# A gated attention and MLP block: means subtracted on GpSimd, weights rounded on VectorE, shares and order of the work set anew

## What is computed

```python
n  = layernorm(x)                                   # over the last axis, no gain or bias
qp = (n @ W1.T + b1) @ W2.T + b2;  kp = (c @ W1.T + b1) @ W2.T + b2
p  = softmax(qp @ kp.T / sqrt(128) + mask)          # mask [128, 120], added
x  = x + tanh(g_xattn) * (p @ c)
h  = relu(q8(q8(layernorm(x)) @ q8w(w1).T + q8w(b1)))   # 128 -> 512
x  = x + tanh(g_ffn) * (q8(h) @ q8w(w2).T + q8w(b2))    # 512 -> 128
# q8: round(16 v) clipped to -128..127, / 16;  q8w: round(64 v) clipped, / 64
```

## Time and profile before

| | |
|---|---|
| runs, us | 66.5, 66.66, 66.83; median 66.66 |
| profiled execution | 66.68 us, span 64.9, granted TensorE clock 1.0 |
| TensorE busy | 57.8 us (89%), weight loads 45.9 |
| VectorE busy | 54.7 us (84%), 308 instructions |
| ScalarE busy | 52.4 us (81%), 145 instructions |
| GpSimd busy | 44.5 us (69%), 92 instructions |
| DMA | 9.09 MB; the load queue is busy until some 20 us |

### The profile page before, as it was taken

How to read it: one execution, slowest core, us unless ns; L and a number is a source line. 1 busy time by engine, 2 the same in 40 slices (tenths; PEclk the granted TensorE clock), 3 DMA queues, 4 the chain that set the end, 5 groups by cost and what they waited for, 6 DMA issues and landing times.

```text
span 64.9 us, 1898 instructions
## 1 busy us (share of the span) xinstructions
PE 57.8 (89%) x565; PEld 45.9 (71%) x565; DVE 54.7 (84%) x308; ACT 52.4 (81%) x145; POOL 44.5 (69%) x92
## 2 busy tenths in 40 slices
PE   4999799768999899999999999999999899996830
PEld 4988574517877788795979899699696779464510
DVE  4569959496999899999799999999999998888620
ACT  2600889849999979999999999999999969769600
POOL 5958888994790894698999999906997949133000
PEclk9999999999999999999999999999999999999999
DMA  0899999999980000000000003120300403041232
GB/s 0 231 412 405 416 414 406 414 400 408 406 324 23 0 0 5 10 0 0 10 0 0 0 5 119 58 111 0 128 34 0 169 8 144 18 162 73 93 121 81
DMA packets 3324, 9.09 MB, mean 140 GB/s; under 512 B 369, under 2 KB 754, under 8 KB 3314
## 3 DMA queue, kind: packets, MB, share of 16 engines
q1 hardware_dynamic: 3312, 8.98, 35.9%
q10 hardware_dynamic: 2, 0.00, 0.0%
HBM read 6.88 MB, written 2.10 MB: 138 GB/s over the span
## 4 chain that ended last, share of the span: by engine, by line
POOL 38%; issue 14%; DMA 14%; ACT 10%; DVE 9%; PE 4%; SPq 4%; POOLq 1%; ACTq 1%; DVEq 0%
POOL xq L377 17%; DMA load_sb<-in_packed 14%; POOL rs L359 12%; ACT pr L597 4%; POOL xn L367 4%; SPq L326 4%; DVE st L641 3%; POOL rs L355 2%; ACT prT L606 2%; PE bank_A L483 2%; DVE load_sb L707 2%; PE bank_O L524 2%; ACT xn L573 1%; DVE mv L644 1%; ACTq L149 1%
## 5 line engine op out<-in xcount | busy, mean ns | idle before, releaser
L624 ACT ACTIVATE h<-bank_H,fb_q 128x512 int8<-128x512 f32 (+2 forms) x28 | 16.2, 645 | 2.2 <-PE bank_H L509 2.1
L641 DVE BATCH_NORM_STATS2 st<-load_sb 128x6 f32<-128x128 f32 x64 | 14.0, 279 | 2.4 <-DMA load_sb<-in_packed 2.3
L359 POOL TENSOR_TENSOR rs<-ve,half 128x4 f32<-128x4 f32 (+2 forms) x9 | 8.5, 941 | 9.3 <-DVE nm L648 9.3
L597 ACT ACTIVATE pr<-sc,mn 128x120 f32<-128x120 f32 x32 | 12.4, 408 | 0.9 <-DVE mn L695 0.9
L377 POOL TENSOR_SCALAR xq<-load_sb,nm,rs 128x128 int8<-128x128 f32 x28 | 12.3, 456 | 0.8 <-POOL rs L359 0.2
L355 POOL TENSOR_TENSOR rs<-ve,half 128x4 f32<-128x4 f32 (+2 forms) x9 | 8.5, 942 | 2.6 <-DVE nm L648 2.6
L367 POOL TENSOR_SCALAR xn<-load_sb,nm,rs 128x128 f32<-128x128 f32 x22 | 9.6, 448 | 0.5
L467 PEld LDWEIGHTS bank_S<-kpT,xaT 128*128 128x128 f32 x64 | 8.1, 191 | 2.6 <-issue 2.3
L483 PE MATMUL bank_A<-load_sb,prT 120*128 120x128 f32 x64 | 9.1, 283 | 0.3 <-ACT prT L606 0.3
L707 DVE SCALAR_TENSOR_TENSOR load_sb<-bank_A,rec,load_sb 128x128 f32<-128x128 f32 x32 | 9.1, 343 | 0.4 <-DVE rec L700 0.3
L524 PE MATMUL bank_O<-w_q,h 128*128 128x128 bf16 x128 | 9.2, 219 | 0.2
(11 more groups left out here) (80 smaller groups left out, 102.0 us busy)
## 6 DMA issues: line engine op xcount, KB each, us to landing
load_sb<-in_packed SPq DMA_DIRECT2D x6, 496.0 KB, 8.0
out_y<-y_sb SPq DMA_DIRECT2D x6, 256.0 KB, 2.0
load_sb<-in_packed SPq DMA_DIRECT2D x2, 512.0 KB, 11.0
load_sb<-in_packed SPq DMA_DIRECT2D x1, 576.0 KB, 14.2
load_sb<-in_packed SPq DMA_DIRECT2D x1, 514.0 KB, 6.1
load_sb<-in_packed SPq DMA_DIRECT2D x1, 448.0 KB, 5.3
load_sb<-in_packed SPq DMA_DIRECT2D x1, 432.0 KB, 12.7
load_sb<-in_packed SPq DMA_DIRECT2D x1, 428.0 KB, 13.3
```

Of the source, the lines that this page charges most:

```text
L359: nc.gpsimd.tensor_tensor(rs2[:, of(g, n=1)], ve2[:, of(g, n=1)], half[:, of(g, n=1)], ALU.pow).then_inc(rs2_done, 1)
L597: nc.scalar.activation(pr[i][:, j, :], sc[i][:, j, :], ACT.Exp, scale=-1.0, bias=mn[:, of(g, j, 1)], accum_out=den[:, of(g, j, 1)]).then_i ...
L624: nc.scalar.activation(low_byte(h16[g % RING], hcols(c, g)), bank_H[c][:, cols(g)], ACT.Relu, bias=fb1_q[:, c:c + 1]).then_inc(h_act[c], 1)
L641: nc.vector.bn_stats(st[:, START[g] + j, :], x_of(g, j)).then_inc(st_done, 1)
```

## The change

Four things. nm is gone from both layer norms; GpSimd subtracts the mean itself, and scale_means computes -mean * rs in one instruction. scale_weights moves, with its three instructions, from ScalarE to VectorE. The shares differ in a few groups: normalise has 21 tiles on GpSimd (22 before), 5 on ScalarE (7), 6 on VectorE (3); quantise 25 on GpSimd (28), 7 on VectorE (4); of the relus 29 are on ScalarE (28) and 7 on VectorE (8). And DUE and FILLERS are new. On VectorE the front is now: stats1 of 0, fold_cp1, scale_means 0, stats1 of 1, fold_cp2, stats1 of 2, scale_means 1, normalise 1, scale_weights, stats1 of 3, row_maxima 0, normalise 2, stats1 of 4, row_maxima 1.

```diff
-XN_ON_POOL = [1, 2, 3, 2, 4, 3, 2, 3, 2]
-XN_ON_ACT = [2, 2, 1, 2, 0, 0, 0, 0, 0]
-XQ_ON_POOL = [1, 3, 4, 4, 4, 4, 4, 3, 1]
-RELU_ON_ACT = [4, 4, 3, 3, 2, 3, 3, 3, 3]
+XN_ON_POOL = [1, 2, 3, 2, 3, 4, 2, 3, 1]
+XN_ON_ACT = [2, 1, 0, 2, 0, 0, 0, 0, 0]
+XQ_ON_POOL = [0, 3, 4, 4, 3, 3, 4, 3, 1]
+RELU_ON_ACT = [4, 4, 3, 3, 3, 3, 3, 3, 3]
...
-    stats1=[375, 485, 715, 977, 1110, 1325, 1569, 2218, 3232],
-    scale_means=[620, 879, 970, 1562],
-    fold_cp1=[627],
-    scale_weights=[845],
-    fold_cp2=[848],
-    copy_keys=[1002, 1053, 1413, 1756, 2149, 2503, 2917, 3552, 4294],
-    row_maxima=[1244, 1470, 1921, 2513, 2868, 3151, 3630, 4255, 4573],
-    normalise_dve=[0, 0, 0, 0, 0, 1789, 2459],
-    quantise_dve=[2032, 2708, 0, 0, 0, 0, 0, 0, 5741],
+    stats1=[380, 590, 743, 1053, 1267, 1505, 1715, 2641, 3361],
+    fold_cp1=[479],
+    scale_means=[583, 868, 0, 1481],
+    fold_cp2=[715],
+    copy_keys=[837, 920, 1332, 1768, 2140, 2719, 3144, 3695, 4263],
+    normalise_dve=[0, 876, 1241, 0, 2144, 0, 2252, 0, 3967],
+    scale_weights=[901],
+    row_maxima=[1180, 1391, 1947, 2306, 2770, 3271, 3555, 4193, 4567],
+    quantise_dve=[2172, 2742, 0, 0, 4256, 4462, 0, 0, 5716],
...
-FILLERS = [8, 38, 19, 5]
+FILLERS = [6, 29, 2, 6, 4]
...
-                pool.wait_ge(ve1_done, 2 * end)
+                pool.wait_ge(ve1_done, end)
...
-                    nc.gpsimd.tensor_scalar(xn[g % RING][:, tile(j)], x_of(g, j), nm1[:, of(g, j, 1)],
-                                            rs1[:, of(g, j, 1)], ALU.add, ALU.mult).then_inc(xn_pool, 1)
+                    nc.gpsimd.tensor_scalar(xn[g % RING][:, tile(j)], x_of(g, j), mv1[:, START[g] + j, 0:1],
+                                            rs1[:, of(g, j, 1)], ALU.subtract, ALU.mult).then_inc(xn_pool, 1)
...
-                nc.vector.tensor_scalar(nm[:, at], mv[:, at, 0], -1.0, None, ALU.mult).then_inc(ve_done, 1)
...
-                dve.wait_ge(ve1_done, 2 * g + 2)
-                nc.vector.tensor_tensor(nr1[:, of(g, n=1)], nm1[:, of(g, n=1)], rs1[:, of(g, n=1)],
-                                        ALU.mult).then_inc(nr1_done, 1)
+                nc.vector.scalar_tensor_tensor(out=nr1[:, of(g, n=1)], in0=mv1[:, of(g, n=1), 0], scalar=-1.0,
+                                               in1=rs1[:, of(g, n=1)], op0=ALU.mult, op1=ALU.mult).then_inc(nr1_done, 1)
...
+            def scale_weights():
+
+                wait_load(dve, "mlp")
+                nc.vector.tensor_scalar(mp_8[:, :], mp_sb[:, :], W_SCALE, None, ALU.mult).then_inc(quant8, 1)
+                dve.wait_ge(row_in, 16)
+                nc.vector.tensor_scalar(fb2_8[:, :], row_sb[:, 2:2 + D], W_SCALE, None, ALU.mult).then_inc(quant8, 1)
+                dve.wait_ge(quant8, 1)
+                nc.vector.tensor_scalar(w1_q[:, :], mp_8[:, 0:C * P], 1.0 / W_SCALE, None, ALU.mult).then_inc(w1_up, 1)
```

More of the change, by code:

```diff
@@ L48 @@
 ]
-XN_ON_POOL = [1, 2, 3, 2, 4, 3, 2, 3, 2]
-XN_ON_ACT = [2, 2, 1, 2, 0, 0, 0, 0, 0]
-XQ_ON_POOL = [1, 3, 4, 4, 4, 4, 4, 3, 1]
-RELU_ON_ACT = [4, 4, 3, 3, 2, 3, 3, 3, 3]
+XN_ON_POOL = [1, 2, 3, 2, 3, 4, 2, 3, 1]
+XN_ON_ACT = [2, 1, 0, 2, 0, 0, 0, 0, 0]
+XQ_ON_POOL = [0, 3, 4, 4, 3, 3, 4, 3, 1]
+RELU_ON_ACT = [4, 4, 3, 3, 3, 3, 3, 3, 3]
 DUE = dict(
-    stats1=[375, 485, 715, 977, 1110, 1325, 1569, 2218, 3232],
[L60 to L63, removed]
-    scale_means=[620, 879, 970, 1562],
-    fold_cp1=[627],
[L66 to L70, removed]
-    scale_weights=[845],
-    fold_cp2=[848],
-    project_keys=[888, 951, 1282, 1638, 2040, 2394, 2796, 3438, 3893],
-    widen_weights=[973],
-    copy_keys=[1002, 1053, 1413, 1756, 2149, 2503, 2917, 3552, 4294],
-    scores=[1069, 1368, 1724, 2126, 2629, 2981, 3528, 4027, 4495],
-    negate_mask=[1157],
-    row_maxima=[1244, 1470, 1921, 2513, 2868, 3151, 3630, 4255, 4573],
[L79 to L86, removed]
-    normalise_dve=[0, 0, 0, 0, 0, 1789, 2459],
-    stats2=[1815, 2325, 2734, 3319, 3711, 4111, 4614, 5031, 5541],
-    copy_base=[1929],
-    rstd2=[1934, 2470, 3171, 3595, 4075, 4257, 4759, 5150, 5641],
-    quantise_dve=[2032, 2708, 0, 0, 0, 0, 0, 0, 5741],
[L92 to L108, removed]
@@ new lines @@
+    spread_gates=[371],
+    stats1=[380, 590, 743, 1053, 1267, 1505, 1715, 2641, 3361],
+    fold_mm1=[386],
+    fold_cp1=[479],
+    rstd1=[492, 728, 926, 1191, 1431, 1643, 1894, 2871, 3524],
+    scale_means=[583, 868, 0, 1481],
+    fold_mm2=[587],
+    normalise_pool=[588, 839, 1302, 1552, 1764, 2110, 2785, 3283, 3797],
+    normalise_act=[603, 990, 0, 1538],
+    transpose_x=[644, 997, 1414, 1845, 2216, 2809, 3248, 3817, 4347],
+    fold_cp2=[715],
+    copy_xT=[735, 1094, 1487, 1910, 2286, 2884, 3318, 3943, 4416],
@@ new lines @@
+    project_keys=[755, 818, 1164, 1558, 1990, 2551, 3033, 3388, 4104],
+    copy_keys=[837, 920, 1332, 1768, 2140, 2719, 3144, 3695, 4263],
+    normalise_dve=[0, 876, 1241, 0, 2144, 0, 2252, 0, 3967],
+    scale_weights=[901],
+    scores=[904, 1266, 1643, 2076, 2468, 3165, 3453, 4016, 4498],
+    copy_ident=[974],
+    gate=[1029],
+    widen_weights=[1046],
+    negate_mask=[1142],
+    row_maxima=[1180, 1391, 1947, 2306, 2770, 3271, 3555, 4193, 4567],
+    exponentials=[1219, 1614, 1986, 2373, 2934, 3425, 3790, 4300, 4723],
@@ new lines @@
+    transpose_probs=[1346, 1734, 2161, 2652, 3116, 3571, 3967, 4460, 4905],
+    fold_base=[1384],
+    copy_probsT=[1400, 1822, 2226, 2776, 3201, 3636, 4040, 4623, 5029],
+    attend=[1469, 1902, 2306, 2856, 3294, 3729, 4147, 4692, 5140],
+    reciprocals=[1473, 1840, 2388, 2632, 3352, 3761, 3956, 4488, 5224],
+    residual=[1637, 2038, 2529, 2984, 3448, 3844, 4290, 4804, 5246],
+    stats2=[1848, 2396, 2851, 3143, 3636, 4066, 4607, 4949, 5422],
+    rstd2=[2005, 2534, 2989, 3413, 3840, 4204, 4745, 5061, 5514],
@@ new lines @@
+    quantise_dve=[2172, 2742, 0, 0, 4256, 4462, 0, 0, 5716],
+    copy_base=[2194],
+    transpose_xq=[2265, 2784, 3536, 4079, 4540, 4880, 5186, 5464, 5735],
+    split_base=[2283],
+    copy_xqT=[2333, 2833, 3739, 4213, 4672, 4979, 5271, 5563, 5813],
+    hidden=[2397, 2942, 3850, 4369, 4757, 5049, 5341, 5628, 5866],
+    relu1=[2524, 3085, 4097, 4505, 4860, 5152, 5444, 5715, 5937],
+    relu0=[2578, 3365, 3980, 4445, 4801, 5093, 5385, 5666, 5899],
+    relu2=[2624, 3576, 4154, 4564, 4920, 5212, 5504, 5764, 5975],
@@ L109 @@
+    quantise_pool=[0, 2645, 3100, 3614, 3961, 4325, 4866, 5167, 5605],
+    relu3=[2671, 3258],
+    mlp_out=[2698, 3614, 4233, 4563, 4927, 5208, 5481, 5767, 5959],
+    result=[3092, 3775, 4395, 4734, 5065, 5357, 5649, 5888, 6077],
+    relu_dve3=[0, 0, 4000, 4499, 4884, 5159, 5504, 5744, 5941],
+    keep_warm0=[370.5],
+    keep_warm1=[586.5],
+    keep_warm2=[643.5],
+    keep_warm3=[754.5],
+    keep_warm4=[996.5],
 )
-FILLERS = [8, 38, 19, 5]
+FILLERS = [6, 29, 2, 6, 4]
 class Share(list):
@@ L215, in norm @@
         def norm(n):
[L216 to L220, removed]
+            return sb(f"st{n}", [P, B, 6]), sb(f"mv{n}", [P, B, 2]), sb(f"ve{n}", [P, B]), sb(f"rs{n}", [P, B])
+        st1, mv1, ve1, rs1 = norm(1)
+        st2, mv2, ve2, rs2 = norm(2)
         mn, den, rec = (sb(n, [P, B]) for n in ("mn", "den", "rec"))
@@ L357, in rstd2 @@
             def rstd2(g):
-                pool.wait_ge(ve2_done, 2 * g + 2)
+                pool.wait_ge(ve2_done, g + 1)
                 nc.gpsimd.tensor_tensor(rs2[:, of(g, n=1)], ve2[:, of(g, n=1)], half[:, of(g, n=1)],
@@ L376, in quantise_pool @@
                 for j in range(XQ_POOL[g]):
-                    nc.gpsimd.tensor_scalar(low_byte(xq16[g % RING], tile(j)), x_of(g, j), nm2[:, of(g, j, 1)],
-                                            rs2[:, of(g, j, 1)], ALU.add, ALU.mult).then_inc(xq_pool, 1)
+                    nc.gpsimd.tensor_scalar(low_byte(xq16[g % RING], tile(j)), x_of(g, j), mv2[:, START[g] + j, 0:1],
+                                            rs2[:, of(g, j, 1)], ALU.subtract, ALU.mult).then_inc(xq_pool, 1)
             def widen_weights():
@@ L553, in gate @@
                 nc.scalar.mul(tg_out[:, :], tg[:, 1:2], 1.0 / (ACT_SCALE * W_SCALE)).then_inc(tg_out_up, 1)
[L555 to L562, removed]
             def copy_base():
@@ L626, in relu @@
                 return stage
-            schedule(once=dict(scale_weights=scale_weights, copy_ident=copy_ident, gate=gate, negate_mask=negate_mask,
+            schedule(once=dict(copy_ident=copy_ident, gate=gate, negate_mask=negate_mask,
                                copy_base=copy_base),
@@ L637, in _, with layer_stats @@
             nc.vector.memset(h16[0][:, :].bitcast(F32), BYTE_PAIR).then_inc(bytes_up, 1)
-            def layer_stats(g, st, mv, ve, nm, scale, st_done, mv_done, ve_done):
+            def layer_stats(g, st, mv, ve, scale, st_done, mv_done, ve_done):
                 for j in range(TILES[g]):
@@ L712, in stats2 @@
                 dve.wait_ge(x2_done, START[g + 1])
-                layer_stats(g, st2, mv2, ve2, nm2, ACT_SCALE, st2_done, mv2_done, ve2_done)
```

(1 more changed line is left out.)

4 lines of the change are left out of this document (2 added, 2 removed).

## The result

The changed kernel takes 72.39 us (median of 4, 72.04 to 73.3) against 66.75 (median of 4): the ratio is 1.082, 95% interval 1.075 to 1.090. Forecast were 65.6 and faster. Its profiled execution took 72.44 us, span 70.6 (before 66.68 and 64.9). Some executions of most kernels here take 1 to 4 us longer than the rest: the ratios, and the executions called undisturbed, leave those out, the medians don't.

What follows compares the result with a forecast made beforehand. The prediction took ScalarE to bound the middle, VectorE close behind, with VectorE's queue in the front setting when it starts. A 1.7 us earlier start, 1.1 of it kept, gave 66.68 - 1.1 = 65.6 us; range 64.7 to 66.6.

Steps and rivals of the forecast that it cites:

- Negated means: Layer norms: VectorE loses 18 instructions, 1.3 us; GpSimd's subtract-and-multiply priced like add-and-multiply, 0.45 us each.
- The upper bound of 1.02: GpSimd's subtract-and-multiply: at most the power's 1.02 us for four elements in place of 0.45.
- The bound: Middle, 14.20 to 49.90 us: ScalarE bounds it, 0.48 us idle, VectorE close behind; GpSimd, 8.14 idle, does not.
- Weights: Front: three weight conversions moved from ScalarE to VectorE cost 1.92 us there, bounds 1.0 and 3.2.
- the third rival: Front: weights on VectorE run at twice the rate, about 1.0 us, first maxima wait only for the mask; 65.2 us, chance 0.2.
- The front made anew: Reordered start: ScalarE's first exponentials at 12.5 instead of 14.22, 1.7 us earlier; third set at 20.0 instead of 21.74.
- The middle: Third exponentials to 49.89: VectorE's net added work 0.65 us; lead kept between 0.65 and 1.56, taken as 1.1.
- The tail: Behind the middle: one relu of group 4 moves from VectorE to ScalarE, cost 0, or 0.58 us if the wait is gone.
- The sum: Whole kernel: 66.68 - 1.1 = 65.6 us, own range 65.0 to 66.0.
- The clock rival: Front: thinner filling halves TensorE's granted clock, keys and scores 2 to 3 us later, 69 us; chance 0.03.

Runs made afterwards that it cites:

- e3: Kernel before, with GpSimd subtracting the negated mean instead of adding it, operand kept: 75.0 and 75.3 us, ratio 1.128.
- e4: Kernel before, with GpSimd adding the mean out of the mean-variance pair instead of the negated mean: 66.65 us in one execution, 68.02 in the other.
- e8: Kernel before plus 48 GpSimd instructions behind all its work, each form three times at 128x128 and 128x512; only the forms' durations count, add-and-multiply 451 and 767 ns.
- e9: Changed kernel with VectorE's negated means restored, GpSimd adding, and TensorE's first instructions in the order of the kernel before: ratio to before 0.992.
- e10: e9 with VectorE writing negated mean and scaled variance by one instruction instead of two: undisturbed 65.6 to 66.0 us, ratio to before 0.986.
- e1: Changed kernel with VectorE writing the negated means again and GpSimd adding them: undisturbed 66.01 and 66.14 us, ratio to before 0.991; four of six 68.7 to 69.2.
- e5: e1 with more matmuls of zeros, FILLERS [6, 37, 14, 6, 14] instead of [6, 29, 2, 6, 4]: undisturbed 66.6 to 67.0 us; 7 of 12 executions long.
- e7: e1 with the three conversions of the MLP's weights back on ScalarE: four executions at 68.8 to 70.7 us.
- e11: e10 with six tiles given from VectorE to GpSimd in the middle: 64.75, 65.06 and 65.47 us, ratio to before 0.975; the other three 68.0 to 68.4.

## Why the prediction was wrong

**Negated means: the step that failed.** "I take no difference" for GpSimd's subtract-and-multiply, at 0.45. It takes 0.79 (0.34 more, 46 times). e3 isolates the operation, e4 clears the operand, e8 shows why the row I priced it from was the wrong neighbour: add-and-multiply is the exception among GpSimd's forms and not their rule. The upper bound of 1.02 held the truth, but I gave it neither a rival nor a part of the range. It would have been 46 x 0.57 = 26 us of GpSimd against 8.1 of idle in the middle: the largest price in the text with no chance at all. The trace of before could have warned: on 96 partitions by 128 columns GpSimd's cast took 0.29 and its tensor_tensor subtract 0.42, so its time already went by the operation.

**The bound.** "Not the bound: GpSimd idle 8.14 us in the middle" told how little GpSimd could bear: of 15.6 us more, the middle's idle took 7.4. And it was a weak reading even of before: idle time doesn't say that the rest of an engine's work keeps nobody waiting. The chain of waits on the page of before puts GpSimd first (line by line, its quantise alone 17%), and the prediction left it out:

```profile
POOL 38%; issue 14%; DMA 14%; ACT 10%; DVE 9%; PE 4%; SPq 4%; POOLq 1%; ACTq 1%; DVEq 0%
```

**Weights: mis-sized, harmless.** 1.23 measured against 1.92. The rates: 0.75 for 1028 columns from SBUF, against 0.741 for 512 from PSUM. By the Trainium skill, "VectorE: DVE Perf Modes", section "The perf-mode tier table", fp32 in SBUF goes at twice the rate; the trace agrees for the large instruction. By the Trainium skill, "SBUF — State Buffer", section "SBUF: two separate sides", such an instruction and one of GpSimd hold a shared pair of ports in turn, and the other waits until the holder's end. The trace agrees in kind, with 1526 ns for the tile beside the three conversions; it doesn't show who held what. In the changed kernel the gain was not had, since the first maxima then waited 0.59 for the mask, as the third rival's text had it.

**The front made anew: right.** Forecast first exponentials 12.5; measured 12.89 in the changed kernel, 12.28 in e9. The key pair was forecast at 7.5 and came at 7.65 in e9, the third exponentials at 20.0 and came at 20.25 in e9 and 20.00 in e10. In the changed kernel they came at 21.58.

**The middle: the size right, the reason not shown.** Forecast lead at the relus of group 4: 1.1. e9, without the slow subtract but with L648 kept, has 0.99 (48.90 against 49.89 in the earlier trace rows); e10, with as few instructions on VectorE as the changed kernel, has 1.01. The prediction had ScalarE do the same work there plus 0.14, and VectorE take the rest of the lead. From the third exponentials to these relus, before, e9 and e10, in the columns of the earlier trace rows:

```profile
21.74:49.89 28.15, 28.15 (x257) 23.76 (x256) 27.02 (x161) 27.70 (x86) 23.17 (x45) 1.00 0.08 28
...
20.25:48.90 28.65, 27.89 (x250) 23.33 (x252) 28.06 (x168) 28.03 (x86) 20.97 (x41) 1.00 0.08 28
...
20.00:48.88 28.88, 28.08 (x251) 23.53 (x253) 28.02 (x160) 28.14 (x87) 21.13 (x41) 1.00 0.08 28
```

In e10 the stretch is 0.73 longer than before, and 0.44 of that is busy time of ScalarE itself (28.14 against 27.70), 0.29 its idle time. VectorE's relief moved the relus of group 4 by 0.02. So more than half of what was given back is ScalarE's own work, put at 0.14; that 1.1 came out so near is in part luck.

**The tail: put at nothing.** So it is in e10 (1.01 ahead at the relus, 1.06 in the span); e9 loses 0.33 there, and the changed kernel is 4.69 late at the relus of group 4 and 5.74 at the last ones.

**The sum.** For the kernel that I believed I was looking at, without L648 and with GpSimd at 0.45, e10 is the nearest: 65.6 to 66.0 against the forecast 65.6. The front and the size of the lead were right, and the price of one operation sank the forecast.

**The rivals.** None had GpSimd. The clock rival, given 0.03, stands closer to the truth than its chance says: not as a cause of this result, whose profile has the full clock from 3.9 us (its key pair took 0.87), but as what the profiles of e1, e5, e7 and e11 show of long executions, which are 5 of 12 or more in every later version of the new front.

## What to carry to other kernels

Price an operation that the trace doesn't show by itself, in a small measurement or as a rival with a chance; a neighbour with the same shape and operands and another operation is no price. On GpSimd prefer one add and one multiply to a pair with a subtract (other pairs were not measured), and pay for the sign elsewhere: a 0.07 us negation on VectorE was cheaper than 0.34 on each of the tiles that use it. When an edit changes operation and operand at once, split them. An engine's idle time doesn't clear it: look at the chain too.

## What the runs showed of the hardware

- GpSimd, float32, 128 partitions, two [128, 1] scalars (e8): add and multiply in either order 0.45 us at 128 columns and 0.77 at 512; subtract and multiply in either order 0.80 and 2.08. One scalar operation alone, add or subtract, is dearer than the pair: 0.61 and 1.57.
- VectorE and GpSimd collide (changed kernel): 1526 ns instead of 788 for a GpSimd tile beside VectorE's conversions of 753, 202 and 414 ns.
- TensorE can work at half speed until some 13 us (e1: the key pair 1.57 us for 0.87, first record of the full clock at 13.07). The clock by stretch reads 1.00 there because no record covers it: matmul durations tell, 241 ns or 196 for a matmul of zeros.
